# Two-phase local outputs and added states in a state-space stage on TensorE

## The reference

```python
z, xBC, dt = split(X @ W_in.T)            # z and x: 1024 channels, B and C: 64 each, dt: 16 heads
dt = softplus(dt + dt_bias)
x, B, C = split(silu(causal_conv4(xBC) + conv_b))
h = 0                                      # per head: 64 channels by 64 states
for t in range(512):
    h = h * exp(dt[t] * A) + dt[t] * x[t] (outer) B[t]
    y[t] = h @ C[t]
y = (y + D * x) * silu(z)
out = rmsnorm(y) * norm_w @ W_out.T
```

## Time and profile before

| | us |
|---|---|
| median of three runs | 2105.48 (2103.21 to 2107.4) |
| span of the profiled execution | 2105.0 |
| of that, state-space stage | 0 to about 873 |
| TensorE busy over the span | 1975.2 (94%) |
| VectorE busy over the span | 1454.4 (69%) |
| ScalarE busy over the span | 1222.7 (58%) |

### The profile page before, as it was taken

One profiled execution on the slowest core, in us unless ns is written; L12 is line 12 of the kernel. 1 busy time (PEld: TensorE's weight loads), 2 busy tenths in 40 slices (PEclk: granted clock), 3 DMA queues, 4 the chain that ended last, 5 costly groups with the idle time before them and its releaser, 6 DMA issues. The chain is left out here.

```text
span 2105.0 us, 40226 instructions
## 1 busy us (share of the span) xinstructions
PE 1975.2 (94%) x13484; PEld 1330.2 (63%) x13484; DVE 1454.4 (69%) x2889; ACT 1222.7 (58%) x3068; POOL 390.2 (19%) x597
## 2 busy tenths in 40 slices
PE   7899999999999999858999999999999999889988
PEld 5667676767676767544566666666665655478853
DVE  7978787878787878526667575757575766555438
ACT  4435353544444444217878787878778786546614
POOL 1110101111111110330222222222222122200006
PEclk9999999999999999878999999999999999999999
DMA  7122222222222222242424343333333332641157
GB/s 214 51 67 72 60 79 60 79 60 79 50 89 50 89 47 72 80 121 56 110 72 122 81 121 81 103 91 105 99 93 100 86 90 78 186 161 61 56 174 270
DMA packets 120051, 200.72 MB, mean 95 GB/s; under 512 B 23088, under 2 KB 44592, under 8 KB 119600
## 3 DMA queue, kind: packets, MB, share of 16 engines
q1 hardware_dynamic: 110640, 179.20, 28.5%
q0 software_dynamic: 9216, 18.89, 3.7%
HBM read 117.27 MB, written 29.88 MB: 70 GB/s over the span
## 5 line engine op out<-in xcount | busy, mean ns | idle before, releaser
L1767 ACT ACTIVATE a_shared<-a_shared,a_mx 128x512 f32<-128x512 f32 x512 | 341.3, 670 | 58.1 <-DVE a_mx L1828 58.0
L1760 ACT ACTIVATE a_probs<-a_scores 128x512 f32<-128x512 f32 x512 | 292.1, 604 | 98.8 <-PE a_scores L1970 96.3
L1828 DVE TENSOR_REDUCE a_mx<-a_shared 128x1 f32<-128x512 f32 x512 | 318.4, 682 | 14.4 <-PE a_shared L1954 13.2
L1970 PE MATMUL a_scores<-a_qs,a_ks 98*128 98x512 f32 x512 | 218.2, 434 | 21.3 <-ACT a_probs L1760 17.6
L1954 PE MATMUL a_shared<-a_ks,a_qs 96*128 96x512 f32 x512 | 214.8, 431 | 19.0 <-ACT a_shared L1767 14.4
L939 PE MATMUL m_proj<-m_xt_hi,link 128*128 128x512 f32 x544 | 225.2, 414 | 5.8 <-DVE m_acc L652 5.6
L1094 PE MATMUL m_outp<-m_wout,m_g 128*128 128x512 f32 x512 | 225.1, 598 | 2.7 <-issue 2.7
L940 PE MATMUL m_proj<-m_xt_lo,link 128*128 128x512 f32 x544 | 215.6, 396 | 0.0
L941 PE MATMUL m_proj<-m_xt_hi,link 128*128 128x512 f32 x544 | 214.3, 394 | 0.0
L467 ACT ACTIVATE m_acc<-m_proj,m_cb,m_cw 128x512 f32<-128x512 f32 x72 | 58.1, 817 | 258.6 <-PE m_proj L941 258.4
L1928 PE MATMUL a_shared<-link 128*128 128x512 f32 x768 | 190.6, 401 | 18.6 <-POOL a_ks L1700 15.7
(11 more groups left out here) (266 smaller groups left out, 3489.9 us busy)
## 6 DMA issues: line engine op xcount, KB each, us to landing
m_dec<-step_decay SPq DMA_DIRECT2D x64, 256.0 KB, 4.1
a_qs<-link SPq DMA_DIRECT2D x256, 64.0 KB, 2.2
m_ce<-run_decay SPq DMA_DIRECT2D x128, 112.0 KB, 3.7
a_ks<-a_k_hi POOLq DMA_DIRECT2D x192, 64.0 KB, 2.4
e_x<-x SPq DMA_DIRECT2D x11, 1024.0 KB, 5.6
m_xt_in<-x_t_in SPq DMA_DIRECT2D x8, 1024.0 KB, 7.9
m_x_tok<-x_in SPq DMA_DIRECT2D x8, 1024.0 KB, 5.6
x<-m_x_tok SPq DMA_DIRECT2D x32, 256.0 KB, 2.2
```

Of the source, the lines that this page charges most:

```text
L1760: act.activation(probs[:, n % 2, h, :], scores[t.score_bank(n, h)][:, :], ACT.Exp, scale=-1.0).then_inc(exp_ready, 1)
L1767: act.activation(scored[:, :], scored[:, :], ACT.Exp, scale=-1.0, bias=mx[:, i % 2, j, h:h + 1], accum_out=den[:, i, j, h:h + 1]).then_inc ...
L1828: dve.tensor_reduce(mx[:, i % 2, j, h:h + 1], bank(what)[:, :], AX.X, ALU.min).then_inc(mx_ready, 1)
L1970: pe.matmul(scores[t.score_bank(n, h)][:, :], ks[0:STACK + 2, t.slot(i), h, j * P:(j + 1) * P], qs[0:STACK + 2, t.slot(i), h, :], start=Tr ...
```

## The change

Both blocks are cut into two phases. In local phase 0 the upper row half writes `yp[0]` while the lower one writes `yp[1]`, with the instructions of the two halves in turn; in phase 1 the banks are swapped. The added states do chunks 0, 5, 2 in phase 0 and 4, 1, 6, 3 in phase 1. Local phase 1 now stands behind the z tile, between the two phases of the added states. The four waits and increments on `even_done` per group become two on `half_done`. Local phase 0 waits until both banks have been read (`y_read` up to 2 gr), where before the second bank's wait came only ahead of the second bank's matmuls. The number of matmuls and all sizes stay.

```diff
+        STATE_PHASES = [(0, 5, 2), (4, 1, 6, 3)]
...
+            def added_states(b, gr, phase):
+                if phase == 0:
+                    weighted = value(pe, at(b, NG, gr + 1))
+                    met(pe, w_used, 1)
+                    pe.wait_ge(xw_ready, weighted)
+                else:
+                    halves = value(pe, at(b, 2 * NG, 2 * gr + 2))
+                    met(pe, w_used, 1)
+                    pe.wait_ge(half_done, halves)
+                for c in STATE_PHASES[phase]:
                     k, half = c // 2, slice((c % 2) * Q, (c % 2 + 1) * Q)
...
-                    if c in (2, 6):
-                        ins.then_inc(even_done, 1)
-                ins.then_inc(st_done, 1)
+                ins.then_inc(half_done if phase == 0 else st_done, 1)
...
+            def local_outputs(b, first, gr, phase):
+                if phase == 0:
+                    gated = value(pe, at(b, XT_TILES, 2 * gr)) if gr or not first else None
...
+                    pe.wait_ge(xdt_ready, scaled)
+                    pe.wait_ge(m_ready, decays)
+                    if gr or not first:
+                        met(pe, w_used, 1)
+                        pe.wait_ge(y_read, gated)
+                else:
+                    halves = value(pe, at(b, 2 * NG, 2 * gr + 1))
+                    met(pe, w_used, 1)
+                    pe.wait_ge(half_done, halves)
+                for k in range(CH):
+                    for h in range(2):
+                        for r in range(2):
+                            j, half = r ^ phase, slice(r * Q, (r + 1) * Q)
+                            ins = pe.matmul(yp[j][h * HP:(h + 1) * HP, k * P + r * Q:k * P + (r + 1) * Q],
+                                            xdt[half, k, 2 * j + h, :], dec[half, gr, 2 * j + h, k * Q:(k + 1) * Q],
+                                            start=(phase == 0 and k == 0), stop=False, skip_group_check=True)
+                if phase == 0:
+                    ins.then_inc(half_done, 1)
...
-                    local_outputs(b, first, gr)
+                    local_outputs(b, first, gr, 0)
                     if gr + 1 < NG:
                         z_tile(b, first, gr + 1, 0)
                     elif more:
                         dt_proj(b + 1, False)
-                    added_states(b, first, gr)
+                    added_states(b, gr, 0)
+                    local_outputs(b, first, gr, 1)
+                    added_states(b, gr, 1)
                     if gr + 1 < NG:
                         z_tile(b, first, gr + 1, 1)
```

More of the change, by code:

```diff
@@ L234, in mamba_stage @@
         bg_read = sem("bg_read")
-        even_done = sem("even_done")
+        half_done = sem("half_done")
         run_ready = sem("run_ready")
@@ L973, in turned_x @@
                     ins.then_inc(xk_done, 1)
[L975 to L980, removed]
+            def added_states(b, gr, phase):
[8 more added lines that the diff above has]
+                for c in STATE_PHASES[phase]:
                     k, half = c // 2, slice((c % 2) * Q, (c % 2 + 1) * Q)
-                    if c % 2 and c != 3:
-                        met(pe, w_used, 1)
-                        pe.wait_ge(even_done, low if c == 1 else high)
                     for j in range(2):
@@ new lines, in added_states @@
+                ins.then_inc(half_done if phase == 0 else st_done, 1)
+            def local_outputs(b, first, gr, phase):
+                if phase == 0:
+                    gated = value(pe, at(b, XT_TILES, 2 * gr)) if gr or not first else None
+                    bg = value(pe, at(b, 1, 1)) if gr == 0 else None
+                    scaled = value(pe, at(b, 2 * NG, 2 * gr + 2))
+                    decays = value(pe, at(b, NG, gr + 1))
+                    met(pe, w_used, 1)
+                    if gr == 0:
+                        pe.wait_ge(bg_read, bg)
+                    pe.wait_ge(xdt_ready, scaled)
[5 more added lines that the diff above has]
+                    halves = value(pe, at(b, 2 * NG, 2 * gr + 1))
+                    met(pe, w_used, 1)
+                    pe.wait_ge(half_done, halves)
[8 more added lines that the diff above has]
+                    ins.then_inc(half_done, 1)
```

## The result

| | before | after |
|---|---|---|
| median of the runs, us | 2105.68 (2103.21 to 2107.4, 4 runs) | 2115.07 (2113.5 to 2117.63, 4 runs) |
| ratio after / before | | 1.0047, 95% interval 1.0034 to 1.0061 |
| profiled execution: span, mean granted clock | 2105.0 us, 0.973 | 2111.8 us, 0.967 |

What follows compares the result with a forecast made beforehand. TensorE, 94% busy, bounds it, with VectorE and ScalarE limiting what savings pass. Six sequences at +1.4 us give +8.5, the last +0.6, less 0.96 for an existing fall: 2105.5 + 8 = 2113.5 us, range 2098 to 2120.

Steps and rivals of the forecast that it cites:

- What the blocks cost: TensorE blocks: local phase 0.6 us, added states 0.97 in both phases, about 1.5 in all behind the z tile.
- the rival that the halves don't overlap: Local outputs: a phase takes 1.0 us, total 2117, up to 2125 with falls; chance 0.08.
- Where the saving goes: Groups 0 to 3: savings ahead of waits become idle time; 0.95 us a sequence gets through at steady clock.
- the steady-clock sum: Whole kernel without new falls: six loop sequences gain 5.7 us, first and last 0.6 together, 6.3 in all.
- What the idle time does to the clock: TensorE's new idle time: clock falls in group 3 of each sequence and in most groups 1.
- most groups 1: Group 1: 1.95 us idle ahead of the z tile brings a clock fall in most sequences.
- Rival 1: Groups 1 and 3: clock stays up, no new falls, only the 6.3 us gain counts, 2099; chance 0.20.
- rival 2: Falls in group 3 only: a sequence gains 0.95 and loses 0.96 us, total 2104.5; chance 0.15.
- Prices: Cost of one clock fall: 0.96 us in group 3, 1.4 us at group 1's z tile.
- The sum: Whole kernel: +1.4 us a sequence, about +8 us over the median before, 2113.5; forecast's chance 0.57.

Runs made afterwards that it cites:

- locals_together: Changed kernel with local phase 1 right behind local phase 0, ahead of the z tile; 2096.89 us, 0.9957 of before.
- less_vector: Changed kernel with VectorE multiplying group 3's decays for one head of four only, output off there; 2094.18 us, 0.9949 of before.
- fill_both: Changed kernel plus unread matmuls in TensorE's waits, 7 in group 1, six and three in group 3; 2097.21 us, 0.9952 of before.
- after_again: Changed kernel, unaltered, run once more beside a third set of runs of before; 2113.30 us, 1.0036 of before.
- before_fill_g3: Kernel before the change plus four unread matmuls in group 3's wait ahead of the local outputs; 2107.54 us, 1.0003 of before.
- fill_g1: Changed kernel plus only the 7 unread matmuls in group 1; 2106.67 us, 1.0000 of before.
- added_only: Kernel before with only the added states in two phases, back to back behind the z tile; 2100.27 us, 0.9967 of before.
- early_filled: Changed kernel, local phases and group 1's added states ahead of the z tile, six unread matmuls in group 3; 2090.35 us, 0.9924 of before.
- together_early: Changed kernel with both local phases, and in group 1 both added phases, ahead of the z tile; 2094.20 us, 0.9944 of before.
- fill_g3: Changed kernel plus only the nine unread matmuls in group 3; 2110.43 us, 1.0021 of before.
- together_filled: Changed kernel, both local phases ahead of the z tile, three unread matmuls in group 1, six in group 3; 2101.64 us, 0.9978 of before.

## Why the prediction was right

**What the blocks cost.** Local phases overlap as foreseen, at 0.69 us instead of 0.6: 32 matmuls pay the same start-up as 56 do, which the 19 ns of the carried outputs had spread over 56. That is 22 ns each with the start-up. The Trainium skill ("TensorE: Matmul & The Clock Gate", the section on 56 against 53.3 ns) has starts never closer than about 25 ns; the 22 ns here, like the 19 of the carried outputs, are under it. What stands behind the z tile came to 1.60 instead of 1.5. Both are terms mis-sized by 0.1, and the rival that the halves don't overlap (block of 1.0) is ruled out. The price of the added states by themselves was further off: 0.97 us foreseen for both phases, 0.66 and 0.67 measured with 0.16 between them (locals_together). In the change this hardly shows, because the three blocks run into each other.

**Where the saving goes.** The wait ahead of the z tile in group 1 was 1.85 us (1.95 foreseen), those of group 3 were 1.75 and 1.02 (1.6 and 1.2). less_vector shows VectorE behind the first one; for group 3 the trace alone names VectorE. At a steady clock a sequence gains 1.0 us (fill_both), 0.95 foreseen. For the whole kernel fill_both's trace has the last carried outputs 8.8 us earlier than before (853.49 against 862.33), where the steady-clock sum had 6.3: it left out the fall at 530.9, 0.96, which fillers take away too, and gave the first and the last sequence 0.6 together, where they came to 0.7 and 1.2. The end of the first sequence is no firm number, though. It was at 110.28 us before and at 108.09 in the kernel after, 2.2 earlier, but at 108.83 in the second trace of the same kernel (after_again), and at 108.94 in before_fill_g3, which has nothing of the change.

**What the idle time does to the clock.** The falls came in group 3 of every sequence of the loop, and in group 1 of all but one, as forecast. In after_again group 3 fell in each of the six again, and group 1 in four of them: in the other two it took 17.62 and 17.63 us at a clock of 1.00. So "most groups 1" was right, and a wait of that size doesn't bring a fall every time. Rival 1 (no falls) and rival 2 (only in group 3) fell with them; fill_both and fill_g1 are what these rivals would have looked like. Rival 1 forecast 2099 and fill_both took 2097.2; rival 2 forecast 2104.5 and fill_g1, with some late starts, took 2106.7.

**Prices.** Group 3: 0.96 foreseen; it took 13.3 to 13.7 us with a fall against 12.46 in fill_both, 0.9 to 1.2, and once 14.78 in after_again. Group 1: 1.4 foreseen, 1.57 measured. The forecast took eight tile matmuls at full clock as 1.99 us, their share of 2.98, and that also holds the start of the first one and the way to the next block. In the spared sequence eight starts take 1.85 us (288.38 to 290.23), at 1.2 GHz 3.38 (395.81 to 399.19), which makes 1.53. That step was right in kind and 0.17 low, 1.0 us over six falls.

**The sum.** Per sequence +1.7 against +1.4. In the two traces the seven sequences behind the first sum to 763.5 against 752.0 us, +11.5, two late starts among them, less 2.2 for the first; the rest of the span, behind this stage, was 2.5 shorter, so the span rose by 6.8. The forecast had +8.1 for those seven and nothing for the other two terms, so that in the traces sequences forecast 3.3 us too cheap were offset by 4.7 us that the working did not have: the closeness of that total is in part luck. The medians differ by 9.4, and by 6.5 when both were run again (after_again); 8 was forecast. The forecast's error is thus of the size by which repeated measurements differ. What was right without luck is the direction, the places of the falls and their price to 0.2 us.

**What the working didn't see.** In the sequence of the kernel after that begins at 217 us the fall came in group 0 (269.5), behind a z tile that waited 1.38 us instead of 0.27. The decays had arrived late there, and group 1 was then spared. And the remedy wasn't in it: the forecast took the idle time as given, where moving one call keeps it out of one piece.

## What to carry to other kernels

Before shortening blocks on a busy engine, find for each block what the engine waits for next; a saving ahead of a wait that another engine sets turns into idle time, and here idle time of 1.85 us in one piece, or 1.75 and 1.02 with 0.69 of work between, mostly cost 0.9 to 1.6 us of half clock. Put the shortened work where the engine waits anyway (ahead of the z tile), even if it overlaps worse there: 3.05 us of work in the right place beat 2.29 in the wrong one by 18 us, nearly all of it falls of the clock that no longer came. To tell a clock effect from a wait, fill the gap with matmuls that nobody reads: what comes back is the clock's share.

## What the runs showed of the hardware that was not expected

**Blocks of one shape run into each other.** Added states and local outputs, both in 64 x 64 quarters but on other banks, overlap in the timeline (399.77 and 400.05 above). The 60 matmuls of the three blocks took 1.60 us together, where the blocks measured alone sum to 0.66 + 0.69 + 0.67 = 2.02. Part of this is that the start-up is paid once: from 56 matmuls in 1.08 us and 32 in 0.69 I estimate it at 0.17 us, 0.34 for the two blocks that save it.

**A transfer that lands early or late.** VectorE's first scan of a sequence waits for the decays that were stored to `step_decay` and come back. Timeline of VectorE in two sequences of the kernel after:

```profile
246.79 2.44 DVE L723 TENSOR_TENSOR_SCAN m_dec<-m_dec,m_delta 128x256 f32<-128x256 f32 x4 [6.22 <-DMA m_dec<-step_decay]
...
354.69 2.44 DVE L723 TENSOR_TENSOR_SCAN m_dec<-m_dec,m_delta 128x256 f32<-128x256 f32 x4 [4.48 <-DMA m_dec<-step_decay]
```

The way from store to scan took either 7.3 to 8.4 us or 8.6 to 9.9, and a late one costs its sequence 0.4 to 1.7 us without any fall, and 2.4 to 2.8 where the clock fell in group 0 as well. Late sequences of seven in each trace: none in before, fill_both, added_only, early_filled and after_again; one in locals_together and less_vector; two in after; three in together_early; four in fill_g1; six in fill_g3, before_fill_g3 and together_filled. It goes with the last two being slower than expected, and could be behind the wide spread of fill_g1 (2101.5 to 2115.3).

The late ones are of two kinds. SyncE, which issues the transfers, reads `step_decay` back when its two stores of decays have landed. Timeline of SyncE in a late sequence of fill_g1, and in one that was in time:

```profile
670.28 0.69 SPq L305 DMA_DIRECT2D step_decay<-m_decay_t  x1
674.97 2.52 SPq L326 DMA_DIRECT2D m_dec<-step_decay  x4
...
455.17 0.69 SPq L305 DMA_DIRECT2D step_decay<-m_decay_t  x1
457.94 2.52 SPq L326 DMA_DIRECT2D m_dec<-step_decay  x4
```

The read was issued 4.69 us after the store in the late one and 2.77 in the other. It is so in all 22 late sequences of fill_g1, fill_g3, before_fill_g3 and together_filled: 3.9 to 4.9 us, against 2.7 to 2.8 in every sequence that was in time. In the one above the other store, `run_decay`, took 3.8 us to land, where it took 1.9 in fill_both. In the seven late sequences of the kernels without fillers the read was issued in time, 2.8 us after the store, and the data came late. So the late issue was seen only with fillers, though not with all (fill_both and early_filled have none), and in one trace of each kernel. What sets either kind stays open; no run here was made for it.
